# Attention block: the second masking is moved to GpSimd and VectorE, and TensorE's part of it is taken out

## The reference

```
h    = relu(layernorm(x))                        # x: 16 x 512 x 512, float32
q,k,v = h Wq + bq, h Wk + bk, h Wv + bv          # 16 heads of 32 features
s    = q k^T / sqrt(32); s = -inf where adj == 0 # adj: 16 x 512 x 512, int32, 0 or 1
out  = x + (softmax(s) v) Wo + bo
```

## Time and profile before

| | us |
|---|---|
| median of three runs | 1732.61 |
| the profiled execution, its own time | 1734.83 |
| its span from first to last instruction | 1733.0 |
| TensorE matmul busy | 1660.5 |
| VectorE busy | 1532.9 |
| ScalarE busy | 1473.9 |
| GpSimd busy | 147.1 |

### The profile page before, as it was taken

One profiled execution on the slowest core, in us unless ns is written; L12 is line 12 of the kernel. 1 busy time (PEld: TensorE's weight loads), 2 busy tenths in 40 slices (PEclk: granted clock), 3 DMA queues, 4 the chain that ended last, 5 costly groups with the idle time before them and its releaser, 6 DMA issues.

```text
span 1733.0 us, 27505 instructions
## 1 busy us (share of the span) xinstructions
PE 1660.5 (96%) x8000; PEld 1035.8 (60%) x8000; DVE 1532.9 (88%) x3653; ACT 1473.9 (85%) x3493; POOL 147.1 (8%) x199
## 2 busy tenths in 40 slices
PE   3899999999999999999999999999999999999987
PEld 2646566566666666666666666666666666656643
DVE  5689898999989899898999989899998999988894
ACT  2688889898898989899898988989888888988983
POOL 0000100101000011100011010010100001110010
PEclk9989999999999999999999999999999999999989
DMA  5434343433434334343333433344343333433311
GB/s 164 116 79 117 88 111 90 113 100 105 108 94 110 91 109 118 101 105 87 112 91 110 118 97 103 90 113 106 104 106 93 111 90 111 119 86 103 87 50 37
DMA packets 118677, 175.17 MB, mean 101 GB/s; under 512 B 32384, under 2 KB 34432, under 8 KB 118528
## 3 DMA queue, kind: packets, MB, share of 16 engines
q1 hardware_dynamic: 114432, 172.35, 37.2%
q10 hardware_dynamic: 4096, 1.06, 0.3%
HBM read 54.79 MB, written 16.78 MB: 41 GB/s over the span
## 4 chain that ended last, share of the span: by engine, by line
PE 76%; DVE 15%; issue 3%; SPq 3%; ACT 2%; DMA 1%; POOL 0%; POOLq 0%; DVEq 0%; ACTq 0%
PE ps L663 14%; PE psO L694 13%; PE ps L674 11%; PE psP L587 11%; PE psP L588 11%; PE psP L589 11%; DVE ps L489 4%; DVE probs L496 4%; PE ps L677 3%; PE ps L635 1%; DVE stats L416 1%; SPq L224 1%; SPq L227 1%; DVE x_tile L424 1%; DVE y_tile L520 1%
## 5 line engine op out<-in xcount | busy, mean ns | idle before, releaser
L489 DVE CUSTOM_DVE_ANT_0 ps<-ps,bias_q 128x512 f32<-128x512 f32 x1024 | 708.4, 693 | 140.2 <-PE ps L663 130.4
L346 ACT ACTIVATE ps<-ps,neg_max 128x512 f32<-128x512 f32 x1024 | 686.8, 671 | 95.9 <-DVE neg_max L489 75.7
L380 ACT ACTIVATE probs<-ps 128x512 f32<-128x512 f32 x1024 | 620.9, 607 | 74.2 <-PE ps L677 72.0
L496 DVE SCALAR_TENSOR_TENSOR probs<-bias_k,probs 128x512 f32<-128x512 bf16 x768 | 550.0, 717 | 6.7 <-ACT probs L380 6.7
L663 PE MATMUL ps<-k_stack,q_stack 96*128 96x512 f32 x1024 | 451.3, 441 | 16.5 <-ACT ps L346 7.8
L674 PE MATMUL ps<-q_stack,k_stack 98*128 98x512 f32 x1024 | 413.8, 405 | 5.1 <-ACT probs L380 4.6
L663 PEld LDWEIGHTS ps<-k_stack,q_stack 96*128 96x128 f32 x1024 | 194.2, 190 | 273.2 <-ACT ps L346 127.6
L694 PE MATMUL psO<-probs,v_sb 128*32 128x512 f32 x2048 | 276.9, 613 | 1.9 <-DVE oT_lo L509 0.9
L674 PEld LDWEIGHTS ps<-q_stack,k_stack 98*128 98x128 f32 x1024 | 196.6, 192 | 45.7 <-ACT probs L380 19.0
L346 ACT ACTIVATION_READ_ACCUMULATOR ps<-ps,neg_max 128x1 f32 x1024 | 217.9, 213 | 0.0
L489 DVE DVE_READ_ACCUMULATOR2_ANT neg_max<- 128x1 f32 x1024 | 143.6, 140 | 0.0
(11 more groups left out here) (60 smaller groups left out, 1920.4 us busy)
## 6 DMA issues: line engine op xcount, KB each, us to landing
q_stack<-part_hi SPq DMA_DIRECT2D x512, 64.0 KB, 2.0
k_stack<-part_hi SPq DMA_DIRECT2D x512, 64.0 KB, 2.0
x_tile<-in_x_dram SPq DMA_DIRECT2D x64, 256.0 KB, 2.9
adj_tile<-in_adj_dram SPq DMA_DIRECT2D x64, 256.0 KB, 3.0
q_stack<-part_lo SPq DMA_DIRECT2D x256, 64.0 KB, 2.0
k_stack<-part_lo SPq DMA_DIRECT2D x256, 64.0 KB, 2.0
y_tile<-in_x_dram SPq DMA_DIRECT2D x64, 256.0 KB, 2.9
out_dram<-y_tile SPq DMA_DIRECT2D x64, 256.0 KB, 2.1
```

The lines of the kernel that those rows point to most:

```text
L346: nc.scalar.activation(item, item, ACT.Exp, scale=-1.0, bias=neg_max[:, g % 2, col:col + 1], accum_out=exp_sum[:, col:col + 1]).then_inc(e ...
L380: nc.scalar.activation(probs[:, n % P_RING, :], ps2[:, n % 2, :], ACT.Exp, scale=SCALE).then_inc(exp2_done, 1)
L489: nc.vector.tensor_tensor_reduce(bank1(("s", u)), bank1(("s", u)), bias_q[:, qt, :], -SCALE, 3.0e38, ALU.add, ALU.min, neg_max[:, g % 2, c ...
L496: nc.vector.scalar_tensor_tensor(out=probs[:, n % P_RING, :], in0=bias_k[:, n % 16 // 4, :], scalar=-MASKED, in1=probs[:, n % P_RING, :], ...
```

## The change

The mask of pass 2 leaves TensorE. Items of key tiles 0 and 2 (n // 4 even) are all masked by VectorE, as line 496 does; items of key tiles 1 and 3 (n // 4 odd) are masked by GpSimd with an int32 product of the bits of `probs` with a new tile `keep_k` (int32, 1 or 0). The key turns still transpose the same data; of each, ScalarE copies the half of the even key tile to `bias_k` (128x512), and VectorE forms `keep_k` from the other half (PSUM bfloat16 to int32). The bank of a key turn is given back only when both have read it. (In the diff, `mask` and the slot loop are GpSimd's, the copy to `bias_k` is ScalarE's, the one to `keep_k` VectorE's; the waits on `bias_k_done` and `keep_k_done` are in `wait_bank1`.) Turn m0 moves from slot 53 to slot 55. GpSimd's queue gets the slot loop of the others. ScalarE's copy no longer waits for `scores2`; PV waits for `even_masked` and `odd_masked` in place of `exp2_done` and `probs_masked`.

```diff
-         24: [("c", 2, -1)], 40: [("c", 3, -1)], 53: [("m", 0, 0)], 56: [("c", 0, 0)], 61: [("m", 1, 0)]}
+         24: [("c", 2, -1)], 40: [("c", 3, -1)], 55: [("m", 0, 0)], 56: [("c", 0, 0)], 61: [("m", 1, 0)]}
...
-        bias_k = sb("bias_k", [P, NT, S], BF16)
+        bias_k = sb("bias_k", [P, 2, S], BF16)
+        keep_k = sb("keep_k", [P, 2, S], I32)
...
+            def mask(b, n):
+                if n % 16 in (4, 12) and n < 16:
+                    pool.wait_ge(keep_k_done, due(2 * b + n // 8 + 1))
+                pool.wait_ge(exp2_done, due(64 * b + n + 1))
+                tile = probs[:, n % P_RING, :].bitcast(I32)
+                nc.gpsimd.tensor_tensor(tile, tile, keep_k[:, n % 16 // 8, :], ALU.mult).then_inc(odd_masked, 1)
+
             def step(k, parity):
...
+                for u in range(SLOTS):
+                    if u == 5: form_rstd(k, 2)
+                    if u == 10: form_rstd(k, 3)
+                    if u == 12: add_bo(k - 2, 2)
+                    if u == 14: add_bo(k - 2, 3)
+                    if u in (44, 45): form_rstd(k + 1, u - 44)
+                    if k == 0 and u == 52:
+                        pool.wait_ge(small_in, 64)
+                    if u in (52, 53): add_bo(k - 1, u - 52)
+                    b, n = pass2(k, u)
+                    if have(b) and n // 4 % 2 == 1:
+                        mask(b, n)
...
                         if kind == "m" and have(k):
                             act.wait_ge(m_turned, due(2 * k + n + 1))
-                            act.wait_ge(scores2, due(64 * (k - 1) + 48 + 8 * n + 8))
-                            act.wait_ge(probs_masked, due(MASKED_ALL * (k - 1) + masked_before(48 + 8 * n + 8)))
-                            nc.scalar.activation(bias_k[:, 2 * n:2 * n + 2, :], bank1((kind, n, rel)).bitcast(BF16).rearrange("p (t q) -> p t q", q=S),
-                                                 ACT.Identity).then_inc(m_done, 1)
+                            act.wait_ge(even_masked, due(32 * (k - 1) + even_before(48 + 8 * n + 8)))
+                            nc.scalar.activation(bias_k[:, n, :], bank1((kind, n, rel)).bitcast(BF16)[:, 0:S], ACT.Identity
+                                                 ).then_inc(bias_k_done, 1)
...
+                elif kind == "m":
+                    dve.wait_ge(bias_k_done, due(2 * b + n + 1))
+                    dve.wait_ge(odd_masked, due(32 * (b - 1) + odd_before(48 + 8 * n + 8)))
+                    nc.vector.tensor_scalar(keep_k[:, n, :], bank1((kind, n, rel)).bitcast(BF16)[:, S:2 * S], 0.0, None, ALU.is_equal
+                                            ).then_inc(keep_k_done, 1)
...
-                    if have(b) and n % 8 in VECTOR_MASKED:
+                    if have(b) and n // 4 % 2 == 0:
...
                     elif kind == "m":
-                        pe.wait_ge(m_done, due(2 * b + n + 1))
+                        pe.wait_ge(bias_k_done, due(2 * b + n + 1))
+                        pe.wait_ge(keep_k_done, due(2 * b + n + 1))
...
-                        last = nc.tensor.matmul(ps2[:, n % 2, :], k_stack[:, g, j, P * kt:P * kt + P], q_stack[:, g, j, :],
-                                                start=True, stop=(n % 8 in VECTOR_MASKED))
-                        if n % 8 not in VECTOR_MASKED:
-                            last = nc.tensor.matmul(ps2[:, n % 2, :], ident_b[:], bias_k[:, kt, :], start=False, stop=True)
-                        last.then_inc(scores2, 1)
+                        nc.tensor.matmul(ps2[:, n % 2, :], k_stack[:, g, j, P * kt:P * kt + P], q_stack[:, g, j, :],
+                                         start=True, stop=True).then_inc(scores2, 1)
...
-                        pe.wait_ge(exp2_done, due(64 * b + 4 * n + 4))
-                        pe.wait_ge(probs_masked, due(MASKED_ALL * b + masked_before(4 * n + 4)))
+                        pe.wait_ge(even_masked, due(32 * b + even_before(4 * n + 4)))
+                        pe.wait_ge(odd_masked, due(32 * b + odd_before(4 * n + 4)))
```

More of the change, by code:

```diff
@@ L34 @@
 P_RING = 8
-VECTOR_MASKED = (0, 1, 2, 4, 5, 6)
 TILES = ([("o", t) for t in range(4)]
@@ L129, in attention_block @@
         bias_done = sem("bias_done")
-        m_turned, m_done = sem("m_turned"), sem("m_done")
+        m_turned, bias_k_done, keep_k_done = sem("m_turned"), sem("bias_k_done"), sem("keep_k_done")
         qkv_done, out_done = sem("qkv_done"), sem("out_done")
@@ L137, in attention_block @@
         scores2, exp2_done = sem("scores2"), sem("exp2_done")
-        probs_masked = sem("probs_masked")
+        even_masked, odd_masked = sem("even_masked"), sem("odd_masked")
         pv_done, o_hi_done, o_lo_done = sem("pv_done"), sem("o_hi_done"), sem("o_lo_done")
@@ L159, in pass2, with even_before, odd_before @@
             return (k, u - S2_AT) if u >= S2_AT else (k - 1, u + SLOTS - S2_AT)
-        def masked_before(n):
-            return n // 8 * len(VECTOR_MASKED) + sum(i < n % 8 for i in VECTOR_MASKED)
-        MASKED_ALL = masked_before(SLOTS)
+        def even_before(n):
+            return n // 8 * 4 + min(n % 8, 4)
+        def odd_before(n):
+            return n // 8 * 4 + max(n % 8 - 4, 0)
         def blocks(step, first=-1):
@@ L287, in add_bo @@
                                             ).then_inc(y_plus_bo, 1)
-            def step(k, parity):
[L290 to L299, removed]
+            def mask(b, n):
[4 more added lines that the diff above has]
+                nc.gpsimd.tensor_tensor(tile, tile, keep_k[:, n % 16 // 8, :], ALU.mult).then_inc(odd_masked, 1)
+            def step(k, parity):
+                for u in range(SLOTS):
[10 more added lines that the diff above has]
+                        mask(b, n)
             blocks(step)
@@ L492, in step @@
                     b, n = pass2(k, u - 1) if u else pass2(k - 1, SLOTS - 1)
-                    if have(b) and n % 8 in VECTOR_MASKED:
+                    if have(b) and n // 4 % 2 == 0:
+                        if n in (0, 8):
+                            dve.wait_ge(bias_k_done, due(2 * b + n // 8 + 1))
                         dve.wait_ge(exp2_done, due(64 * b + n + 1))
-                        nc.vector.scalar_tensor_tensor(out=probs[:, n % P_RING, :], in0=bias_k[:, n % 16 // 4, :], scalar=-MASKED,
+                        nc.vector.scalar_tensor_tensor(out=probs[:, n % P_RING, :], in0=bias_k[:, n % 16 // 8, :], scalar=-MASKED,
                                                        in1=probs[:, n % P_RING, :], op0=ALU.add, op1=ALU.min
-                                                       ).then_inc(probs_masked, 1)
+                                                       ).then_inc(even_masked, 1)
                     if u in C_AT:
@@ L670, in step @@
                             pe.wait_ge(c_in, due(32 * (4 * b + g + 1)))
-                        if g == 0 and j == 0:
-                            pe.wait_ge(m_done, due(2 * b + kt // 2 + 1))
                         pe.wait_ge(exp2_done, due(64 * b + n - 1))
-                        last = nc.tensor.matmul(ps2[:, n % 2, :], k_stack[:, g, j, P * kt:P * kt + P], q_stack[:, g, j, :],
-                                                start=True, stop=(n % 8 in VECTOR_MASKED))
-                        if n % 8 not in VECTOR_MASKED:
-                            last = nc.tensor.matmul(ps2[:, n % 2, :], ident_b[:], bias_k[:, kt, :], start=False, stop=True)
-                        last.then_inc(scores2, 1)
+                        nc.tensor.matmul(ps2[:, n % 2, :], k_stack[:, g, j, P * kt:P * kt + P], q_stack[:, g, j, :],
+                                         start=True, stop=True).then_inc(scores2, 1)
                     project(k, u)
```

## The result

The changed kernel takes 1780.17 us (median of four runs, 1777.06 to 1781.23) against 1735.38 for the kernel before: ratio 1.0247, interval 1.0216 to 1.0277, 45 us slower. The forecast was 1718 with a range of 1686 to 1767.

A forecast was written before the change was run, and what follows sets the result against it. It took TensorE as the bound. Per graph -3.0 + 2.5 - 0.8 + 0.4 = -0.9 us, -14 over 16 graphs, took the profiled 1734.8 to 1720, and the runs' median, 2 lower, to 1718 us; range 1686 to 1767.

The forecast's parts named there:

- The bound: TensorE sets the pace in slots without turns; a graph takes 103.0 us, 5.5 of them turns and real waits.
- the mask matmuls: Removing TensorE's mask matmuls saves 0.23 us each, for 13 of 16 in a graph: 3.0 us a graph.
- m0 at slot 55: Slots 53 to 56: item 56 waits for the exponential, item 57 for `keep_k`; +2.5 us a graph, ends 0 and 3.5.
- Collisions: GpSimd's products and VectorE's two-input operations hold each other up: 0.4 us a graph, ends 0 and 2.2.
- 0.8 forecast at slots 12 and 13: Waits around turns h2 and h3 shrink as a mask leaves VectorE: 0.8 us a graph saved, ends 0 and 1.2.
- GpSimd: Each int32 product takes 1.28 us, 655 us in all; four end 2 us ahead of PV.
- The sum: All terms of a graph added: -0.9 us, -14 for 16 graphs, giving 1718 us.
- full gain: Rival: m0's chain costs little and VectorE's relief holds; 40 to 60 us gained, 1673 to 1692 us; chance 0.18.
- The slow product: Rival: GpSimd's product takes 2.1 us, so PV waits on `odd_masked`; 1795 us; chance 0.15.
- the lock: Rival: products collide with VectorE, 1.1 us reaching TensorE twice a graph; 1747 us, with a third 1765; chance 0.17.

The follow-up runs named there:

- no_pe_mask: The kernel before without its 256 mask matmuls on TensorE, items 3 and 7 of each eight left unmasked: 1700.83 us, ratio 0.9805.
- filler: The changed kernel with 6 matmuls of 128x512 ahead of item 56 and 6 ahead of item 57 in each graph: 1744.31 us, ratio 1.0038.
- y_later: The changed kernel with GpSimd's y additions of tiles 0 and 1 at slots 60 and 61 instead of 52 and 53: 1740.56 us, ratio 1.0026.
- tail_fill: m0_back_y_later with two further matmuls of 128x512 in each slot from slot 29 of the step behind the last graph: 1683.16 us, ratio 0.9696.
- tail_dve: m0_back_y_later with VectorE also doing GpSimd's products in the last 32 items of the last graph: 1684.75 us.
- m0_back_y_later: The changed kernel with turn m0 back at slot 53 and the y additions at slots 60 and 61: 1688.74 us, ratio 0.9722.
- both edits at the end: The edits of tail_fill and tail_dve together on m0_back_y_later: 1681.48 us, ratio 0.9688.
- move_only: The kernel before with turn m0 at slot 55 instead of 53, all masks as before: 1775.17 us, ratio 1.0224.

## Why the prediction was wrong, step by step

**The bound, and the mask matmuls: right in the main.** 0.225 us each where 0.23 was taken, and the other slots give back 2.57 of 3.0 us a graph. In no_pe_mask, where VectorE keeps all its masks, a whole graph gave only 1.8: how much of the price reaches the time hangs on what else a slot waits for. (In the reading of the earlier trace rows, 2.27 us is the one slot with PV, not two; the sums use it rightly.)

**The step that failed is "m0 at slot 55".** Its mechanism held: item 56 behind the exponential of item 55 behind the copy, item 57 behind keep_k. Its size, +2.5 us a graph with an upper end of 3.5, should have been +5.5. 2.44 of the missing 3.0 is the clock. The forecast left out what idle time does to TensorE's clock; it priced the waits as lost time only. filler shows it: 36 us less with the idle time filled, against a loss of 45. The Trainium skill reports the like of another kernel (TensorE: Matmul & The Clock Gate, A second HAM failure mode: psum-queue depth-cycling): a TensorE that idles a little and often while it cycles through PSUM banks can make its clock swing. This case agrees, with 0.85 and 0.55 in two neighbouring stretches. The rest is the length of the first wait, 4.05 for 3.23 us, which y_later puts on the collision just ahead of it; the mean of slots 53 to 56 before, 6.98 where 6.7 was read from one graph, takes a part of that back.

**Collisions: mechanism right, the 0.4 us taken for them too small.** It said that two y additions come "just behind 52". They cost 0.8 at item 56, where three c operations in a row are held; the forecast named these operations but priced no chain of them. Slots 8 to 11 grew by 0.7 (6.71 to 7.43), most of it in slot 11; there a mask that meets product 12 takes 1.56 us. That also took half of the 0.8 forecast at slots 12 and 13: slot 12 fell from 1.80 to 1.28, as forecast, but slot 11 grew from 1.60 to 2.07.

**GpSimd: right.** 1309 ns against 1280; PV waited for a product 3 times, 2.7 us in all.

**The end of the run: missed.** The sum had graphs only. The end grew by 10 us. Both the clock (tail_fill) and the products (tail_dve) have a part in it; how it divides stays open, since in no_pe_mask the end grew as much with no product at all.

**The rivals.** None holds as written. The slow product's time, 1795, is the nearest to the measured one, but the product was not slow; the lock's 1747 to 1765 had a true mechanism and lacked the clock. The condition of the "full gain" can be had by undoing the move: that gives 29 us, and 47 with the y additions out of the way. Its own sum (3.1 to 3.8 us a graph, 50 to 61 in all) gives 1673 to about 1684, not 1692.

## What to carry to other kernels

A wait on TensorE, where it is the bound, has two prices: the time, and the clock that it may lose for some us after it. In this kernel one wait of 1.4 to 1.7 us was enough in some graphs, and with a second one of 0.95 us behind it the low stretch was twice as long as without its last 0.6 us; where a new order makes such waits, price the clock too. Read the bank list for every turn that is moved, and put GpSimd's work where VectorE has no short chain that others wait for. The fastest version here is m0_back_y_later with both edits at the end: 1681.48 us, ratio 0.9688 (0.9669 to 0.9707) to the kernel before; with the added matmuls alone it is as fast within the noise.

## What was not expected of the hardware

- The clock decides by little: 0.8 us less waiting in a graph (y_later) took the time at the low level from 92 to 10 us, and in move_only the same wait of 3.92 us between two items lost it in 5 of 12 graphs and not in 7.
- With fewer matmuls a stretch became longer: in the profiled execution of no_pe_mask the end of the run went from 53.6 to 62.7 us, clock 0.91 to 0.66. That is one execution against one, and added matmuls (tail_fill) took 6.1 us off the same stretch of m0_back_y_later.
- A one-input VectorE operation on 16 columns, SBUF to SBUF (line 451), is held by a GpSimd instruction too: 1.21 us instead of 0.17.
- An int32 product on GpSimd costs what a float32 sum does: median 1288 and 1304 ns for 128x512.
